# Ring units made ahead of the tile passes in a graph-attention kernel of four layers

## The reference

```python
x = _layernorm(x + _L0_gnn_ref(x, adj, ...))      # e = leaky(s_src[i] + s_dst[j]), mask, softmax, @ h, elu
x = _layernorm(x + _L1_gnn_ref(x, adj, ...))      # the same with another slope and a bias
x = _layernorm(x + _L2_gnn_ref(x, adj, ...))      # 8 heads: q.k/8 + bias, leaky, mask, softmax, @ v, @ Wp
# layer 3
s = u[:, :, None, :] + v[:, None, :, :]           # 1024 x 1024 x 64 per graph
s = jnp.where(s > 0, s, ALPHA * s)
e = jnp.einsum('bijf,f->bij', s, a[:, 0])
e = jnp.where(adj > 0, e, NEG_INF)
h_prime = jnp.einsum('bij,bjf->bif', softmax(e), hp)
x = _layernorm(x + elu(h_prime))
```

## Time and profile before

| | |
|---|---|
| Time, median of 2 runs | 8485.54 us (8483.6 to 8487.48) |
| The profiled execution | 8497.64 us, span 8495.8 us, mean granted TensorE clock 0.981 |
| Busy, share of the span | PE 92%, VectorE 88%, ScalarE 87%, GpSimd 18% |
| Chain that ended last, by engine | PE 53%, VectorE 16%, no wait shown 14%, ScalarE 13% |
| Largest groups | ring units on ScalarE 4021 us, ring matmuls 3920 us, ring units on VectorE 3379 us |

### The profile page before, as it was taken

The page is one execution under the profiler, slowest core; times in us unless marked ns, Lnnn a source line. Parts: engine busy times, 40 slices in busy tenths (PEclk is TensorE's granted clock), DMA queues, the critical chain, the costliest instruction groups (busy, mean ns, idle before and its releaser), DMA issues.

```text
span 8495.8 us, 175156 instructions
## 1 busy us (share of the span) xinstructions
PE 7806.9 (92%) x64968; PEld 3570.9 (42%) x64968; DVE 7445.0 (88%) x10867; ACT 7388.3 (87%) x8641; POOL 1519.0 (18%) x582
## 2 busy tenths in 40 slices
PE   4889999899999999989899999999989999899998
PEld 2535344353443534435353443534435344353442
DVE  4789898898988989889898888988889898898888
ACT  3699888898888898889888888988889888898888
POOL 1212121121211112121121211212112121111000
PEclk8999999999999999999999999999999999999999
DMA  3626254362543625335253452624426254362430
GB/s 81 166 56 148 65 122 96 75 151 56 123 93 84 142 61 125 89 84 131 60 136 78 98 119 59 146 68 114 104 65 150 62 122 96 78 150 56 107 72 20
DMA packets 501426, 830.78 MB, mean 98 GB/s; under 512 B 89890, under 2 KB 155426, under 8 KB 500514
## 3 DMA queue, kind: packets, MB, share of 16 engines
q1 hardware_dynamic: 500514, 818.85, 41.5%
HBM read 76.25 MB, written 4.19 MB: 9 GB/s over the span
## 4 chain that ended last, share of the span: by engine, by line
PE 53%; DVE 16%; issue 14%; ACT 13%; SPq 2%; DMA 2%; DVEq 0%; ACTq 0%; POOL 0%; POOLq 0%
PE psum L871 23%; PE psum L784 9%; PE psum L746 7%; DVE work L1472 7%; ACT work L1130 6%; PE psum L742 4%; ACT work L994 4%; ACT work L985 3%; PE psum L765 2%; PE psum L677 2%; DVE work L1280 2%; DVE work L1308 2%; SPq L549 2%; DMA work<-work 1%; PE psum L672 1%
## 5 line engine op out<-in xcount | busy, mean ns | idle before, releaser
L1130 ACT ACTIVATE work<-v,ucol 128x1024 f32<-128x1024 f32 x3727 | 4021.4, 1141 | 318.8 <-PE psum L871 317.2
L871 PE MATMUL psum<-work,pick 128*32 128x512 f32 x32768 | 3919.9, 605 | 294.9 <-DVE top L1423 132.1
L1472 DVE TENSOR_SCALAR work<-v,ucol 128x1024 f32<-128x1024 f32 x4465 | 3379.1, 809 | 293.2 <-PE psum L871 265.7
L871 PEld LDWEIGHTS psum<-work,pick 128*32 128x32 f32 x32768 | 930.8, 110 | 2520.2 <-issue 1983.3
L1280 DVE CUSTOM_DVE_ANT_0 work<-psum,work 128x1024 f32<-128x1024 f32 x1280 | 1538.0, 1202 | 324.2 <-ACT work L985 304.4
L1308 DVE STREAM_TRANSPOSE work<-work 128x1024 f32<-128x1024 f32 x1280 | 1583.8, 1237 | 70.6 <-DMA work<-work 68.6
L994 ACT ACTIVATE work<-work,least 128x1024 f32<-128x1024 f32 x1280 | 1464.2, 1144 | 4.5 <-DVE least L1280 4.4
L985 ACT ACTIVATE work<-psum,beta 128x1024 f32<-128x1024 f32 x1024 | 1139.0, 1112 | 325.8 <-PE psum L746 267.4
L784 PEld LDWEIGHTS psum<-work,vw 128*64 128x64 f32 x16384 | 878.3, 137 | 613.8 <-issue 605.1
L784 PE MATMUL psum<-work,vw 128*64 128x128 f32 x16384 | 1119.7, 279 | 8.0 <-DMA work<-work 8.0
L742 PE MATMUL psum<-mask,ident_b 128*128 128x512 bf16 x2560 | 780.1, 387 | 236.8 <-DVE least L1280 181.5
(11 more groups left out here) (159 smaller groups left out, 5010.0 us busy)
## 6 DMA issues: line engine op xcount, KB each, us to landing
work<-work SPq DMA_DIRECT2D x2560, 256.0 KB, 4.6
adj_in<-in_adj SPq DMA_DIRECT2D x128, 512.0 KB, 4.6
tile3T<-blocks SPq DMA_DIRECT2D x512, 128.0 KB, 2.7
x_in<-in_x SPq DMA_DIRECT2D x16, 256.0 KB, 4.6
xT_both<-in_xT SPq DMA_DIRECT2D x16, 256.0 KB, 5.3
out<-yout SPq DMA_DIRECT2D x16, 256.0 KB, 2.6
work<-in_WqT SPq DMA_DIRECT2D x1, 128.0 KB
work<-in_WkT SPq DMA_DIRECT2D x1, 128.0 KB
```

The costliest lines, as they stand in the source:

```text
L871: mm = pe.matmul(score3[32 * q:32 * q + 32, cols], pick[:, 15 - kk:47 - kk], ring[u % RING][q][:, cols], start=(kk == 0), stop=(kk == 15), ...
L1130: ins = act.activation(ring[u % RING][q], v3[:], ACT.Relu, bias=ucol[:, 4 * T + q, kk:kk + 1])
L1472: ins = dve.tensor_scalar(ring[u % RING][q], v3[:], ucol[:, 4 * T + q, kk:kk + 1], 0.0, ALU.add, ALU.max)
```

## The change

In slots that have a ring step, ScalarE and VectorE make the ring units of the next step first and do the tile passes behind them. In slots without a ring step, and in the prologue, the order is as it was. `first_of` stays in front on both engines; `exp3`, `last_top` and the copies stay behind. Nothing is added or removed, PE's and SP's programs are the same, and so is the planner's split of the units.

```diff
@@ ScalarE, layer3
                 for s in range(SLOTS):
                     T, kk = of_step(s)
+                    if more and kk is None:
+                        tiles(g + 1, it, s)
                     if more:
-                        tiles(g + 1, it, s)
                         first_of(it, s)
                     if s == 3:
                         column_3(it)
                     if kk is not None and STEPS[s] + 1 < GROUPS:
                         ring_units(g, STEPS[s] + 1, more)
+                    if more and kk is not None:
+                        tiles(g + 1, it, s)
@@ VectorE, slots
                 for s in at:
                     T, kk = of_step(s)
+                    if a is not None and (g is None or kk is None):
+                        tiles(a, it, s, flagged)
                     if a is not None:
-                        tiles(a, it, s, flagged)
                         first_of(a, it, s)
                     if g is not None and s == 4:
                         column_3(g, it)
                     if g is not None and kk is not None:
                         if STEPS[s] + 1 < GROUPS:
                             ring_units(g, STEPS[s] + 1, a is not None)
+                        if a is not None:
+                            tiles(a, it, s, flagged)
                         last_top(g, it, s, tail)
```

## The result

The changed kernel takes 9093.25 us (2 runs, 9074.69 to 9111.81) against 8485.54 us: a ratio of 1.071 with a 95% interval of 1.067 to 1.076. It is slower, as forecast, but by 7.1% and not by 3.9%; 9093 lies outside the range of 8590 to 8900. Its profiled execution took 9074.69 us, with a span of 9072.9 us and a mean granted clock of 0.967 (0.981 before).

What follows compares the result with a forecast made beforehand. No single bound overall, but PE in layer 2's 179 us stretch; 5.3 + 4 + 2.3 + 10.5 = 22.1 us a period, times 15 = 332 us, on 8497.6 gives 8830, less 12: 8817 us. Range 8590 to 8900.

Steps and rivals of the forecast that it cites:

- ordinary pairs: Layer 2, pairs without another turn-buffer use between tiles: no cost, slack of leaky shrinks from 2.8 to about 0.8 us.
- Slots 84 to 134 without the q copies: Slots 84 to 135 of layer 2: ten places with slack below the delay, 10.5 us a period, bounds 5 and 13.
- Layer 0: Slots 8 to 17: units ahead of relu wait for the ring step; +5.3 us a period, bounds 2 and 6.
- Layer 1: Slots 38 to 47: same start and loop as layer 0; PE 4 us late at ring step 48, bounds 1 and 5.
- Slots 64 to 82: Layer 2, slots 66 to 82: PE waits at even tiles; +2.3 us a period, bounds -2 and +4.
- the loop: Layer 0: ring step s-2, units, relu, leaky, then S(s) and ring step s; both engines 2.8 us late by slot 13.
- over 2 us: Sign in the changed profile: values_3, in slot 14 of layer 0, waiting over 2 us; before, 0.81 us.
- Moved past nothing else: Claim of no further cost: last_top keeps its place, SP's program is untouched, a pair's move is issued 1 to 2 us later.
- The slack: Rival, chance 0.25: PE has room or the waits overlap with existing ones, so no change over 2%.
- Faster: Rival, chance 0.03: PE's 160.9 us of waits for ring units end and layer 2's starting hole fills, 8293 us.
- The loops: Rival, chance 0.06: units wait for ring steps in layer 2 too, up to 30 us a period, 8935 us.
- The rule by the busy share of weight loads: In the 179 us stretch, PE's 55% would make ScalarE or VectorE the bound and drop the 10.5 us; the prediction rejected it.

Runs made afterwards that it cites:

- e4: Kernel before, with the new order only in slots from 64 on, without the six slots of the q copies: 8707.76 us, ratio 1.026.
- e7: Kernel before, with the new order only in thirteen slots of layer 2 where leaky had 2.1 to 3.3 us of slack: 8518.36 us, ratio 1.0037.
- e3: Kernel before, with the new order only in slots below 64 (tile passes of layers 0 and 1): 8629.85 us, ratio 1.017.
- e1: Changed kernel, with the q copies behind the tile passes in slots 83, 84, 101, 102, 119 and 120: 8839.39 us, ratio 1.042.
- e9: Kernel before, with the q copies ahead of the tile passes in their six slots, ring units still last: 8617.45 us, ratio 1.015.

## Why the prediction was right and wrong

**Right: that it is slower, and by what.** PE's slack in ordinary pairs shrinks and holds. In the changed kernel, slots 106 to 110 (compare):

```profile
1919.61 1.23 DVE L1283 CUSTOM_DVE_ANT_0 work<-psum,work 128x1024 f32<-128x1024 f32 x1 [0.50 <-ACT work L985]
...
1922.12 0.38 PE L742 MATMUL psum<-mask,ident_b 128*128 128x512 bf16 x1 [0.16 <-issue]
...
1923.38 2.08 DVE L1475 TENSOR_SCALAR work<-v,ucol 128x1024 f32<-128x1024 f32 x3
...
1925.37 1.24 DVE L1311 STREAM_TRANSPOSE work<-work 128x1024 f32<-128x1024 f32 x1
...
1926.53 1.18 DVE L1283 CUSTOM_DVE_ANT_0 work<-psum,work 128x1024 f32<-128x1024 f32 x1
...
1927.79 0.61 PE L742 MATMUL psum<-mask,ident_b 128*128 128x512 bf16 x2 [1.42 <-DVE least L1283]
```

`leaky` of slot 106 ends at 1920.84 and S(108), one of whose records is missing, starts by 1922.12 without a wait for it: some 1.1 us of slack where 0.8 was forecast and 2.8 had been. Behind it three units, the transpose, then `leaky` of slot 108, and S(109) waits 1.42 us (1.6 forecast). It starts 5.9 us behind S(108); forecast 6, before 4.4.

**The terms that held.** Slots 84 to 134 without the q copies: forecast 10.5 us a period in ten places, measured 11.1 (e4: 11.6). Place by place, forecast and then measured: 84 and 86, 1.3 and 0.7; 90, 1.0 and 0.8; 94, 1.8 and 1.5; 108, 1.6 and 1.3; 112, 1.0 and 1.1; 116, 0.8 and 0.6; 126 to 130, 3.0 and 3.3. That is 9.3 us in the places named. Another 1.5 us come from slots 100 and 124, where units take longer beside GpSimd (e7) and nothing had been forecast. So the mechanism held, and that the sum fits within 0.6 us is partly luck.

Layer 0: forecast 5.3, measured 5.7. Layer 1: forecast 4, measured 3.5. e3 has the same two numbers with nothing else changed, so these losses are shown to come from these slots. Slots 64 to 82: forecast +2.3, measured 0.8 here and up to 2.2 in e1, within the 3 us by which that row moves anyway. In layer 0 the sum was right and its split was not. I had both engines 2.8 us late by slot 13 and the end, `values_3`, bringing the other half. Measured, PE was 4.8 us late by the ring step of slot 11 and 5.2 by that of slot 14; the loop cost more and the end less:

```profile
1588.93 2.73 PE L686 MATMUL psum<-linT_s,xTa 65*128 65x64 f32 x16 [1.24 <-DVE least L1283]
```

`values_3` waits 1.24 us for `leaky` (0.81 before), less than the "over 2 us" that I named as a sign. The four terms were 22.1 us in the forecast and sum to 5.7 + 3.5 + 0.8 + 11.1 = 21.1 us.

**The step that failed: "Moved past nothing else".** The missing 17.0 us of 38.3 lie in the three pairs of slots with q copies. I had written that `first_of` stays in front. In front of the units, yes; but before it stood *behind* the tile passes, and the diff puts it ahead of them. So the tile passes were moved past two things, and I walked the one. The timeline of the changed kernel, slots 82 and 83:

```profile
1813.50 1.11 ACT L1018 ACTIVATE q_hi<-psum,q_bias 128x1024 fp32r<-128x1024 f32 x1 [3.51 <-PE psum L708]
1814.51 2.17 ACT L1130 ACTIVATE work<-v,ucol 128x1024 f32<-128x1024 f32 x2
1814.64 1.28 DVE L1274 SCALAR_TENSOR_TENSOR q_lo<-psum,q_bias,q_hi 128x1024 fp32r<-128x1024 f32 x1 [3.32 <-ACT q_hi L1018]
...
1815.85 1.59 DVE L1475 TENSOR_SCALAR work<-v,ucol 128x1024 f32<-128x1024 f32 x2
1816.59 1.10 ACT L985 ACTIVATE work<-psum,beta 128x1024 f32<-128x1024 f32 x1
...
1818.52 1.18 DVE L1283 CUSTOM_DVE_ANT_0 work<-psum,work 128x1024 f32<-128x1024 f32 x1
...
1819.77 1.22 PE L708 MATMUL psum<-xTa,Aq 64*128 64x512 f32 x1 [3.44 <-DVE least L1283]
```

ScalarE waits 3.51 us for the first `make_q` with tile passes ready behind it; VectorE waits 3.32 us for ScalarE. Only then come units, relu, transpose and `leaky`, which frees the buffer for the second `make_q`. PE waits 3.44 us for it. Then a second cost follows, which stands in no term of my sum: the matmuls after this wait take 1.22 us and not 0.69, as the clock granted to PE has fallen to its lower level (0.98 over 1812 to 1819 us, 0.53 over 1819 to 1826). In e1 the same place has no wait in front of `make_q`:

```profile
1781.22 0.69 PE L720 MATMUL psum<-xTa,Aq 64*128 64x512 f32 x1
```

In e9 the wait is 1.93 us in all 45 of these places (three in each of 15 periods). In 27 of them the clock stays up; in 18 it falls, during `make_q` or the ring step behind it. One place of each kind:

```profile
1212.41 0.69 PE L711 MATMUL psum<-xTa,Aq 64*128 64x512 f32 x1 [1.93 <-DVE least L1286]
...
1213.47 1.92 PE L874 MATMUL psum<-work,pick 128*32 128x512 f32 x16
```

```profile
1743.85 0.69 PE L711 MATMUL psum<-xTa,Aq 64*128 64x512 f32 x1 [1.93 <-DVE least L1286]
...
1745.18 3.30 PE L874 MATMUL psum<-work,pick 128*32 128x512 f32 x16
```

16 ring matmuls take 1.92 us in the first and 3.30 in the second. In the changed kernel the waits in these places are 3.3 to 4.1 us, and the clock falls in 44 of the 45. So the two parts of the 17.0 us can be told apart in the trace: PE's waits for `leaky` in front of the second `make_q` are 10.9 us a period (nothing before), and the rest, some 6 us, is matmuls at the lower clock. In e9 it is 5.8 us of these waits and some 2 us of slower matmuls, of 8.5. In the other rows of the changed kernel the added time is waits, to within 1 us.

**The range was too narrow for the same reason.** Its upper end, 8900, came from the bounds of terms that I had found; a term that I hadn't found had no bound. With the q term, 17.0 x 15 = 255 us, the forecast of 8817 would have been 9072.

**The rivals.** The slack does not hold everywhere (ratio 1.071). *Faster* was right in one detail: PE's waits for ring units in layer 1, 2.5 us a period, did end, and they are the 38 us by which the row of 160.9 us shrank; the others lie in slots that don't change, and in layer 1 new waits cost more than the 2.5 us. The loops did not run away in layer 2: e4 shows 11.6 us in slots 84 to 134 and not 30. (That rival's price was also added up wrong: 36 slots at 1.1 us are 40 us a period, not 30, and the 179 us stretch has 27 ring steps, not 33.) The rule by the busy share of weight loads, read as a measure of what bounds these 179 us, would have covered PE's new waits there. It didn't: between slots 84 and 134, the places of `make_q` left out, PE's waits grew by 12.0 us a period and the period by 11.1, as the gapless distances of the earlier trace rows had said. The Trainium skill (Perfetto Trace Analysis, Identifying the Most-Contended Engine) gives that share as a measure of the distance to the roofline; in these 179 us, 55% busy by it, it did not tell that PE was the bound.

## What to carry to other kernels

When a piece is moved in a hand-written order, write down the whole order of each engine before and after, and go through every pair that has changed places, the small pieces also: here the pair that nobody spoke of (tile passes and q copies) cost 255 of 577 us. An engine without gaps can be hurt at places where two uses of a buffer follow close together, and these can be found and priced one by one from the slack in the trace (10.5 us forecast for ten places, 9.3 measured in them). A new wait on the matrix engine can cost more than itself: here 10.9 us of waits brought some 6 us of slower matmuls. Work of two engines that slow each other, as VectorE's units and GpSimd's mask work do here, has to be priced in the place to which it is moved.

## What the runs showed of the hardware

Ring units of VectorE beside GpSimd's mask conversion take up to 4.17 us for three, and 2.08 with nothing beside them; so a reordering can change durations that it doesn't touch. In the trace of the kernel before, none of the 3645 units that ran with GpSimd idle took more than 0.76 us; of the 820 beside a GpSimd instruction 324 took over 0.9, up to 2.63. The Trainium skill (SBUF — State Buffer, Who interferes with whom) has the two engines share a pair of ports, which VectorE takes for a `tensor_scalar` in its two-port modes and which the engine that comes first holds for its whole instruction; this would do it. The traces agree in that every long unit stands beside GpSimd work, and no run here shows the ports themselves or the mode.

Waits on PE of 1.9 to 4.1 us in front of `make_q` were followed by matmuls at the lower of the two clock levels in 18 of 45 places when the wait was 1.93 us (e9), and in 44 of 45 when it was 3.3 to 4.1 us (the changed kernel): 1.22 us for a piece of 0.69 us, up to 3.64 us for a ring step of 1.92. The 1.42 us wait at slot 109 was followed by matmuls of the usual length (0.61 us for its first two).
